# Block-quantised feed forward and latent attention joined into one stage, the causal mask added on VectorE

## What is computed

```python
# layer 0, feed forward (blocks of 32 along the last axis share a power of two)
gate = q_act(x) @ q_w(w_gate).T            # 256 -> 1024
up   = q_act(x) @ q_w(w_up).T              # 256 -> 1024
x = layernorm(x + q_act(silu(gate) * up) @ q_w(w_down).T)
# layer 1, latent attention, 16 heads, causal
q = rmsnorm(x @ q_a_w, q_a_ln_w) @ q_b_w                   # 192 -> 16 x (128 + 64)
kv_raw = x @ kv_a_w                                        # 64 latent, 16 x 64 rope keys
kv = rmsnorm(kv_raw[..., :64], kv_a_ln_w) @ kv_b_w         # 16 x (128 keys + 128 values)
scores = where(causal, (q . k) / sqrt(192), -big)
x = layernorm(x + (softmax(scores) @ v) @ o_w)
```

## Time and profile before

| | us |
|---|---|
| median of 3 runs | 1354.85 |
| the profiled execution | 1354.72 |
| its span, first to last instruction | 1352.9 |
| self attention and first cross attention | 0 to about 426 |
| quantised feed forward, first reduction to last normalise | 431.0 to 573.9 |
| latent attention, first turn of x to last stores | 579.6 to 1054 |
| second cross attention and mixture feed forward | from 1056.6 |

### The profile page before, as it was taken

How to read it: one execution, slowest core, us unless ns; L and a number is a source line. 1 busy time by engine, 2 the same in 40 slices (tenths; PEclk the granted TensorE clock), 3 DMA queues, 4 the chain that set the end, 5 groups by cost and what they waited for, 6 DMA issues and landing times. The chain is left out here.

```text
span 1352.9 us, 27646 instructions
## 1 busy us (share of the span) xinstructions
PE 1080.3 (80%) x9056; PEld 830.0 (61%) x9056; DVE 852.3 (63%) x2220; ACT 594.7 (44%) x1306; POOL 506.5 (37%) x975
## 2 busy tenths in 40 slices
PE   4778899568885566469999999999998588858997
PEld 3556676335552222269898998988987255535665
DVE  3468997368884999824444444444443488856886
ACT  2345555258884333223223332233321388854553
POOL 5256788623332344312322233222331333322232
PEclk8889999879997877879999999999998699989999
DMA  8799998255552411110100111001010555521111
GB/s 157 150 178 216 213 178 157 63 139 128 139 139 52 91 47 47 34 64 21 29 24 24 31 30 32 23 23 31 23 32 16 133 130 139 135 67 38 47 58 39
DMA packets 138274, 112.13 MB, mean 83 GB/s; under 512 B 16848, under 2 KB 130816, under 8 KB 138176
## 3 DMA queue, kind: packets, MB, share of 16 engines
q1 hardware_dynamic: 124864, 100.01, 31.4%
q10 hardware_dynamic: 11344, 8.72, 2.3%
q0 software_dynamic: 1968, 2.16, 1.0%
HBM read 68.91 MB, written 31.52 MB: 74 GB/s over the span
## 5 line engine op out<-in xcount | busy, mean ns | idle before, releaser
L389 DVE TENSOR_REDUCE ca_nm<-ca_p_s 128x2 f32<-128x512 f32 x256 | 168.3, 684 | 44.4 <-PE ca_p_s L298 42.3
L529 ACT ACTIVATE ca_pt<-ca_p_e 128x512 f32<-128x512 f32 x256 | 139.4, 595 | 10.2 <-PE ca_p_e L318 4.4
L318 PE MATMUL ca_p_e<-ca_qs,ca_ks 128*128 128x256 bf16 x512 | 100.1, 278 | 52.3 <-ACT ca_pt L529 50.4
L298 PE MATMUL ca_p_s<-ca_ks,ca_qs 96*128 96x256 bf16 x512 | 103.6, 287 | 30.9 <-DMA ca_ks<-k_stack 30.9
L2118 ACT ACTIVATE la_pq<-la_p_s,la_nm 128x128 f32<-128x128 f32 x256 | 72.9, 368 | 106.3 <-DVE la_nm L2158 106.3
L1951 PE MATMUL la_p_f<-la_qt,q_w 128*128 128x128 f32 x512 | 101.4, 280 | 12.5 <-ACT la_lt L2099 11.3
L1952 PE MATMUL la_p_f<-la_qt,q_w 128*128 128x128 f32 x512 | 99.0, 275 | 0.0
L521 ACT ACTIVATE ca_qs<-ca_p_m 32x1024 bf16<-32x1024 bf16 x64 | 65.0, 1016 | 74.2 <-PE ca_p_m L308 73.4
L1951 PEld LDWEIGHTS la_p_f<-la_qt,q_w 128*128 128x128 f32 x512 | 77.6, 192 | 16.3 <-ACT la_lt L2099 16.3
L318 PEld LDWEIGHTS ca_p_e<-ca_qs,ca_ks 128*128 128x128 bf16 x512 | 40.3, 98 | 76.3 <-ACT ca_qs L521 64.3
L61 POOL TENSOR_TENSOR la_kk<-la_lt,one 64x1024 f32<-64x1024 f32 x32 | 60.4, 1889 | 65.7 <-ACT la_lt L2099 64.4
(11 more groups left out here) (275 smaller groups left out, 2834.2 us busy)
## 6 DMA issues: line engine op xcount, KB each, us to landing
sa_qks<-sa_qkp SPq DMA_DIRECT2D x96, 128.0 KB, 5.2
ca_qs<-q_stack SPq DMA_DIRECT2D x32, 384.0 KB, 4.7
ca_ks<-k_stack SPq DMA_DIRECT2D x32, 384.0 KB, 5.6
ca_ct<-in_ctx_t SPq DMA_DIRECT2D x32, 128.0 KB, 5.4
ca_xr<-x_state SPq DMA_DIRECT2D x32, 128.0 KB, 2.1
x_state<-ca_xn SPq DMA_DIRECT2D x32, 128.0 KB, 2.0
k_stack<-sa_cxp SPq DMA_DIRECT2D x16, 192.0 KB, 3.1
q_stack<-sa_parts SPq DMA_DIRECT2D x16, 192.0 KB, 2.5
```

The lines of the kernel that those rows point to most:

```text
L298: last = pe.matmul(p_s[n % 3][:, qc, :], QS[b % 3][0:STACK, h, 128 * qc:128 * qc + 128], KS[b % 3][0:STACK, h, :], start=True, stop=True)
L318: last = pe.matmul(p_e[h % 2][:, kc, :], KS[(2 * i + u) % 3][:, h, 128 * kc:128 * kc + 128], QS[(2 * i + u) % 3][:, h, :], start=True, sto ...
L389: dve.tensor_reduce(NM[u][:, h, :], p_s[(H * (2 * i + u) + h) % 3][:, :, :], AX.X, ALU.max, negate=True).then_inc(max_done, 1)
L529: act.activation(PT[h // 4][:, h % 4, :, :], p_e[h % 2][:, :, :], ACT.Exp, scale=SCALE).then_inc(exp_done, 1)
```

## The change

One stage, `mx_latent_attention`, takes the place of both. Every engine's queue is a list of steps c = -4 to 15, all straight code. Step c does the rest of attention item c, the front of attention item c + 1, the second half of feed forward item c + 2 (inner turned, down, residual, normalise), the first half of item c + 3 (x turned, gate, silu, up, inner), and the quantising of x of item c + 4.

- The normalised rows of the feed forward (`XM`, three buffers) stay in SBUF and are read by `f0` and as the attention's residual. The store to `x_state[2]` and the attention's two loads of each item are gone.
- PSUM: the attention has six banks (`p_t` is one bank now, so `turn_exps` waits for the copy of the group before), the feed forward two (`p_m`). Gate, up, turned inner, turned x and down share these two: `ups` starts after silu has read the gates.
- The inner product of item c + 3 and the x of item c + 4 are quantised as one tile of 1280 columns (`quantize(k, steps)`), its seven steps spread over VectorE's queue. POOL scales the 1024 columns of inner in one instruction.
- The mask matmul is gone. `maxima` adds the mask to the scores on the way to SBUF (`MS`), then takes the maximum out of `MS`; `exps` reads `MS`. The next scores wait for the add (`masked`) and not for the exponentials.
- `turn_exps(c + 1, 0)` and `copy_exps(c + 1, 0)` move from the start of an item's step to the end of the step before, on TensorE ahead of `project(c)`.
- Silu and the exponentials now alternate on ScalarE within a step.

The core of the diff (the bodies of the functions that only change their indices are left out):

```diff
-def mx_feed_forward(nc, sh, x_in, x_out, experts_in):
...
-def latent_attention(nc, sh, x_in, x_out, q_out, q_a_in, kv_a_latent_in, kv_a_rope_in):
+def mx_latent_attention(nc, sh, x_in, x_out, q_out, experts_in, q_a_in, kv_a_latent_in, kv_a_rope_in):
...
+            def ups(m):
+                for f in range(2):
+                    pe.wait_ge(silu_done, 2 * m + f + 1)
...
+            def turn_inner(m):
+                pe.wait_ge(inner_scaled, m + 1)
+                if real(m + 1):
+                    pe.wait_ge(inner_done, 2 * (m + 1) + 1)
...
-                wait(pe, exp_done, n - 1)
-                pe.matmul(p_s[g % 2][:, :, :], sh.identb[:, :], sh.mask_qk[:, :, :], start=True, stop=False,
-                          skip_group_check=True)
+                wait(pe, masked, n - 1)
                 for j in range(4):
...
-                wait(pe, p_copied, n - 1)
+                wait(pe, p_copied, n)
...
+            def step(c):
+                now, later, inner, gate = real(c), real(c + 1), real(c + 2), real(c + 3)
+                (TensorE's order, each with its condition)
+                f0(c + 1) turn_x(c + 3) scores(c, 2) turn_exps(c, 1) weigh(c, 0) gates(c + 3) f1(c + 1)
+                scores(c, 3) weigh(c, 1) rope(c + 1, 0) turn_exps(c, 2) ups(c + 3) rope(c + 1, 1) weigh(c, 2)
+                turn_exps(c, 3) f4(c + 1) turn_inner(c + 2) queries(c + 1, 0) weigh(c, 3) queries(c + 1, 1)
+                down(c + 2) queries(c + 1, 2) queries(c + 1, 3) scores(c + 1, 0) turn_heads(c, 0)
+                turn_heads(c, 1) scores(c + 1, 1) turn_exps(c + 1, 0) project(c)
...
+                (ScalarE's order)
+                f0(c + 1) copy_x(c + 3) exps(c, 2) f1(c + 1) silu(c + 3) exps(c, 3) rope0(c + 1) f4(c + 1)
+                copy_inner(c + 2) queries(c + 1, 0) queries(c + 1, 2) exps(c + 1, 0) f9(c) exps(c + 1, 1)
...
+            def quantize(k, steps):
+                part = grid_part(k)
...
+                    if s == HALF_STEP:
+                        wait(dve, x_scaled, min(k, B))
+                        wait(dve, inner_scaled, k - 1)
+                    mx_step(dve, s, XI[k % 2][:, part], w).then_inc(grid_steps, 1)
...
+            def maxima(b, g):
+                n = G * b + g
+                dve.wait_ge(scores_ready, n + 1)
+                wait(dve, exp_done, n - 1)
+                dve.tensor_tensor(MS[g % 2][:, :, :], p_s[g % 2][:, :, :], sh.mask_qk[:, :, :], ALU.add).then_inc(masked, 1)
+                dve.wait_ge(masked, n + 1)
+                dve.tensor_reduce(NM[b % 2][:, 4 * g:4 * g + 4], MS[g % 2][:, :, :], AX.X, ALU.max,
                                   negate=True).then_inc(max_done, 1)
...
+                (VectorE's order, k = c + 4)
+                maxima(c, 2) copy_exps(c, 1) normalise(c - 1) divide(c, 0) maxima(c, 3) norm_qa(c + 1)
+                divide(c, 1) copy_exps(c, 2) inner(c + 3) rope1(c + 1) divide(c, 2) quantize(k, (0,))
+                copy_exps(c, 3) quantize(k, (1, 2, 3)) divide(c, 3) quantize(k, (4,)) queries(c + 1, 1)
+                quantize(k, (5, 6)) mx_residual(c + 2) queries(c + 1, 3) maxima(c + 1, 0)
+                mx_normalise(c + 2) f10(c) maxima(c + 1, 1) copy_exps(c + 1, 0) residual(c)
...
+                (POOL's order)
+                rstd(c - 1) scale_inner(c + 2) rms(c + 1) split(c - 1) place_latent(c + 1) scale_x(c + 4)
+                mx_rstd(c + 2)
...
+                (SP's order)
+                store(c - 1) load_x(c + 6) load_residual(c + 4)
```

More of the change, by code:

```diff
@@ L1380 @@
 MX_STEPS = 7
+PRODUCT_STEP = 4
 HALF_STEP = 5
@@ L2151, in _, with step @@
-            over_pairs(act, pair)
+            def step(c):
+                now, later, inner, gate = real(c), real(c + 1), real(c + 2), real(c + 3)
+                if later:
+                    f0(c + 1)
+                if gate:
+                    copy_x(c + 3)
+                if now:
+                    exps(c, 2)
+                if later and now:
+                    f1(c + 1)
+                if gate:
+                    silu(c + 3)
+                if later and not now:
+                    f1(c + 1)
+                if now:
+                    exps(c, 3)
+                if later:
+                    rope0(c + 1)
+                    f4(c + 1)
+                if inner:
+                    copy_inner(c + 2)
+                if later:
+                    queries(c + 1, 0)
+                    queries(c + 1, 2)
+                    exps(c + 1, 0)
+                if now:
+                    f9(c)
+                if later:
+                    exps(c + 1, 1)
@@ new lines, in quantize @@
+            def quantize(k, steps):
+                part = grid_part(k)
+                blocks = slice(part.start // MX, part.stop // MX)
+                w = {what: tile[:, blocks if what in ("top", "inverse", "half") else part] for what, tile in grid.items()}
+                for s in steps:
+                    wait(dve, grid_steps, MX_STEPS * k + s)
+                    if s == 0 and k < B:
+                        dve.wait_ge(xi_loaded[k % 2], 16 * (k // 2 + 1))
+                    if s == 0 and k:
+                        dve.wait_ge(inner_done, 2 * k)
+                    if s == HALF_STEP:
+                        wait(dve, x_scaled, min(k, B))
+                        wait(dve, inner_scaled, k - 1)
+                    mx_step(dve, s, XI[k % 2][:, part], w).then_inc(grid_steps, 1)
@@ L2261, in _ @@
+            for c in range(-AHEAD, B):
+                step(c)
+            normalise(B - 1)
         @block.gpsimd
@@ L2321 @@
+            for c in range(-AHEAD, B):
+                step(c)
+            rstd(B - 1)
+            split(B - 1)
 EXPERTS, EI = 8, 176
```

964 lines of the change are left out of this document (406 added, 558 removed).

## The result

The changed kernel takes 1261.97 us, the median of 4 runs (1260.3 to 1264.32), and the kernel before took 1355.09 beside it (1354.7 to 1361.38). The ratio is 0.930, 95% interval 0.927 to 0.934: faster by 93 us, 14 more than the 79 forecast. The profiled execution took 1264.32 us, its span 1262.2.

What follows compares the result with a forecast made beforehand. VectorE bounds the feed forward, TensorE the attention and the joined stage. Fill 49, steps 0 to 12 409.5, then 29.3, 28.2 and 20.9 sum to 536.9 us against 616.2, giving 1275.5, range 1255 to 1304.

Steps and rivals of the forecast that it cites:

- rival C: Joined stage: TensorE's waits vanish and the step is 29.3 us, total 1247 (to 1263); chance 0.10.
- fill: Start of the joined stage, from its first reduction until step 0 begins at 480: 49 us.
- 13 steps: Steps 0 to 12, which carry all the work of both halves: 31.5 us each, 409.5 together.
- step 13: Near the stage's end, a step without gates: 29.3 us.
- step 15: Last attention item: 20.36 before, less turned exponentials and masks, plus two masked adds on its chain: 20.9 us.
- TensorE's sum: TensorE's work in one joined step without any wait, counted from matmul rows: 29.3 us.
- The walk: One step traced through the engines' queues: waits of 0.35, 0.15 and 1.35 us on TensorE, step 31.15.
- POOL's 0.35: VectorE held beside POOL's scaling and placing; 0.15 and about 0.2 us reach TensorE, making the step 31.5.
- A (table switch): ScalarE's two table changes per step delay the rope copy or more: total 1285 or 1294 us; chance 0.13.
- B (VectorE's order): VectorE's queue order becomes the bound, adding 2 us per step: total 1301 (1290 to 1315); chance 0.17.
- D (clock in the step): TensorE's clock falls to its lower level inside steps, making the kernel slower, 1379 us at 8 us; chance 0.05.
- E: A wait across steps serialises the two halves: 37.7 us per step, total 1356; chance 0.03.

Runs made afterwards that it cites:

- e5: Kernel before with the attention's hardware loop written out as straight code, nothing else: 1346.85 us, ratio 0.996.
- e4: Changed kernel with the projection ahead of the first turned exponentials, and the heads' copies moved ahead: 1255.42 us, ratio 0.925.
- e7: Changed kernel with VectorE's three small quantising steps behind the last division instead of before it: 1260.14 us, ratio 0.931.
- e10: Changed kernel with the edits of e4 and e7, and the attention's normalise behind the division of group 0: 1245.60 us, ratio 0.921.
- e6b: Changed kernel with VectorE's rounding of 1280 columns done twice, the first time into a spare tile: 1268.36 us, ratio 0.937.
- e3: Changed kernel with silu replaced by a copy, so no table switches in the stage: 1259.83 us, ratio 0.929.
- e6a: Changed kernel with VectorE's block reduction of 1280 columns done twice, the first time into a spare tile: 1284.21 us, ratio 0.949.
- e11: Kernel of e10 with unused matmuls on a spare bank filling TensorE's waits in the last item: 1242.20 us, ratio 0.918.
- e1: Changed kernel with the mask put back on TensorE as a matmul, all else the same: 1253.84 us, ratio 0.925.

## Why the prediction was right, and where it was not

The time came out 13.5 us under the sum of 1275.5, inside the range of 1255 to 1304. It is also 1 us under what the prediction called its own forecast (1263 to 1286), in the bracket of rival C (to 1263), and the step of 30.38 lies just outside the 30.5 to 32.3 that it named as the sign of being wrong. So the mechanism was right and the waits were sized too long. The stretch was forecast at 536.9 us and measured at 520.7. By terms:

| term | forecast | measured | difference |
|---|---|---|---|
| fill | 49 | 52.6 (82.98 from first reduction to first residual add, less one step) | +3.6 |
| 13 steps | 13 x 31.5 | 13 x 30.38 | -14.6 |
| step 13 | 29.3 | 29.34 | 0 |
| step 14 | 28.2 | 27.78 | -0.4 |
| step 15 | 20.9 | 16.09 | -4.8 |

That makes -16.2. The late start of the stage, which no term had, gives back 5.2, and 1275.5 - 16.2 + 5.2 is the profiled 1264.3 within 0.3.

*TensorE's sum.* 29.3 without waits, measured 29.14. The counting of moved matmuls by their rows was right to 0.2. Step 13, without gates, is 27.43 less its waits, where the sum less gate and up gives 27.6; that its 29.34 equals the forecast of 29.3 is luck, for a wait of 0.66 before a weighing is in it that nobody had walked. I took nothing for the straight code, with 0.2 per item as the bound, and e5 shows 0.5, of which 0.3 is shorter waits and 0.2 is not. Those 0.2 are as large as the sum's error, and the 0.3 may be part of why the waits came out shorter than walked; no run shows that in the joined stage.

*The walk.* It named the one long wait, its place and its cause: masked maximum, exponentials, the turning ahead of the projection. Measured 1.05, forecast 1.35. It stands at the turning itself, as the walk's own times have it (exponentials 0 end at 30.5, 1.15 behind scores 1), though the list of signs put it before the projection on the heads' copy. The copy ends at 667.33 and the projection starts at 667.40, so both conditions bind; e4 moved both. The smaller waits were 0.19 for 0.35 and none for 0.15. In all 1.24 for 1.85, which is 0.6 of the 1.12 us that the step was too long; POOL's 0.35 and the sum's 0.2 are the rest. The engines' sums were near: VectorE busy 24.0 us per step for 24.9, ScalarE 14.3 for 14.1. The stage has the 28 table loads that were forecast.

*POOL.* I gave it 0.35 on the path. The holds are there, and the small step's is near the size I allowed (1.76 of up to 1.9; normalise 0.915 in the median of 0.403 to 1.085), but nothing of the largest reached TensorE: e7 removed it and the step stayed at 30.37. The normalise's wasn't removed by itself in this order; the list has no wait of TensorE behind it. They matter once the long wait is gone: in e4 the held normalise stands ahead of the division that TensorE waits for, and moving it behind the division (e10) removed that wait. The Trainium skill (SBUF — State Buffer, section SBUF: two separate sides) would have the scaled product, with two SBUF inputs, held too. No run here shows it: in none of the profiles does the product run beside a POOL instruction. In this step it starts at 658.35 where the placing ends at 657.84, so its 1.48 us says nothing on that rule.

*The last step.* I priced step 15 by the earlier trace rows, where the projection took 6.30 at a fallen clock, and didn't ask whether the clock would fall again. In the changed kernel it stayed at 1.00 and the projection took 3.69. e6b, with the same last item at a fallen clock, took 21.04, so 20.9 was right for that case. The term should have carried both ends; the 4.8 are the state of the clock, not an error in the work.

*The fill.* 3.6 too short. In it the normalise of the feed forward's first item took 2.00 us beside POOL's scaling, where the fill was priced without holds, and the granted clock was 0.68; the two aren't told apart.

*The rivals.* A (table switch): the activation follows each load by 0.01 us, ScalarE was ahead of its consumers, and e3 shows the price on the path as nothing. The Trainium skill (ScalarE: Activation LUTs, section What ACT_TABLE_LOAD costs) has about 1283 ns for the load, and the mean of 24 loads here is 1283; of the drain of some 1380 ns for every switch this trace shows nothing. B (VectorE's order): not the case at 30.38, but e6a shows how close it was, 1.4 of the next 1.5 us at that place would have been paid. C (no waits, 1247 to 1263): its range holds the measured 1261.97, but not its mechanism, since 1.24 us of waits are left in the step; e10 and e11 reach 1245.6 and 1242.2 by other orders. D (clock in the step): 1.00 throughout, waits of 1.05 notwithstanding; only the last step's clock differs between profiles. E: no, VectorE's and TensorE's work overlap in every step.

*The mask.* The forecast didn't price this part by itself: it took 0.86 off TensorE in one sentence and let the later maximum lengthen a wait in another. Set beside each other (1.35 of waiting for 0.54) they already said that it nearly cancels. e1 makes it a loss of 0.26 per step.

## What to carry to other kernels

When work moves from the bound engine to an idle one, look whether it lands on a chain on which the bound engine then waits, and reorder that chain in the same edit; the same masked add lost 0.26 us per step in one order of the queues and gained 0.21 in another. An engine's idle share says nothing of its slack at one place of its queue: 1.48 us added at one cost 1.40 per step, 0.83 at another nothing. The step without its waits came within 0.2 us of TensorE's sum of matmuls, so that sum, counted from rows, is the first estimate to make, and the waits are the second. To price a wait, compare the starts of blocks with and without it: the listed idle time can be less than what the step pays (0.28 listed, 0.51 paid).

## What was new about the hardware

- Two table loads per step, of 1.28 us each, with the next activation 0.01 us behind each; taking all 24 away changed no step.
- A two-item hardware loop over five queues cost 0.5 us per item against the same code written out (28.30 against 27.82 us).
- Four exponentials with a bias out of SBUF take 1.28 us, out of PSUM 1.14 (390 against 368 ns each, with the next one overlapping).
- VectorE's int32 step on 128x40, 0.185 us alone (e7), took 1.757 beside POOL's placing of the latent and ended when that did (657.89 and 657.84 us):

```profile
653.94 3.90 POOL L61 TENSOR_TENSOR la_kk<-la_lt,one 64x1024 f32<-64x1024 f32 x2 [4.45 <-ACT la_lt L1875]
656.13 1.76 DVE L1429 TENSOR_SCALAR mx_g_inverse<-mx_g_top 128x40 int32<-128x40 int32 x1
```

- An idle time listed before a weighing was less than what it cost: 0.28 for 0.51 us per step (e4 against e10), 1.2 for 1.40 (e6a).
- TensorE's clock over the last 10 us of the stage is 1.00 in seven of the 14 profiles and 0.55 to 0.61 in the other seven, with nearly the same code and waits before it.
